# Windowed attention in a fused layer: the softmax division goes from GpSimd onto a diagonal matrix built by VectorE

## Chip, cores and metric

The kernel runs on all 8 cores of one Trainium2 chip. Each core takes one of the 8 sequences (4096 tokens of 1024 features) with the whole set of weights; nothing is exchanged between cores. The metric is device time in microseconds (us) of the slowest core.

## The reference

```python
xn = layernorm(x)                                 # no gain, no bias
q, k, v = split(xn @ w_qkv)                       # 16 heads of 64
s = (q * 64 ** -0.5) @ k.T                        # key j counts for query i if i-255 <= j <= i
a = softmax(s) @ v
g, u = xn @ w_gate.T / 127, xn @ w_up.T / 127     # int32 weights, 3072 hidden
y = x + a @ w_out + (silu(g) * u) @ w_down.T / 127
```

## The kernel before

A core's 32 tiles of 128 tokens are worked in two halves of 16. Each half has an attention phase (A), tile by tile, and then the feed-forward part (phase B) twice, once for each half of the 3072 hidden features. Weights of phase A and of phase B share one region of SBUF, `wreg`: `wq_sb` lies at bytes 0 to 49151 of each partition and `wo_sb` behind it; `wg_sb` (8 pieces of 3072 bytes), `wu_sb` (8 more) and `wd_sb` (12 of 2048 bytes) lie over the same bytes. Loads convert from float32 or int32 to bfloat16 on the way and are issued from the GpSimd queue (`load_attn_weights`, `load_ffn_weights`).

The program is written by hand in the order of the engines' queues. `Sched.add` appends an operation to the queue of one engine and works out its waits from the buffers that it reads and writes; `_wkeys` cuts `wreg` into blocks of 512 bytes, so that a load waits for the last matmul that reads just its own bytes. TensorE alone does not wait for its own earlier work; a VectorE operation that reads a result of VectorE does wait for it.

`phase_a_tile` does this for a tile:

- 128 matmuls (L394) for Q and K in 16 feature chunks of 128 columns (`fc`), 8 matmuls (`d`) each, then 16 of 512 columns for V (L419), which read `wq_sb` row block by row block;
- the transposes of the next tile's normalised input (L369);
- a software pipeline over 8 pairs of heads, in 13 steps. In step s: `pair_softmax` of pair s-1, `pair_scores` of pair s, `pair_transpose` of pair s-3, `pair_av` of pair s-4, and in steps 8 to 12 the output projection (L439).

The score banks are P0 to P4 (head modulo 5), the transposed probabilities go to P5 (even head) and P6 (odd head), the values product to P7. `pair_softmax` has two row maxima on VectorE (L258), two exponentials with their sums on ScalarE (L264), two reciprocals on VectorE (L271) and two multiplications of the 128x384 probabilities by the reciprocals on GpSimd (L277, `mprobs`). `pair_transpose` multiplies each 128x128 block of `mprobs` with the identity (L285) and copies the bank to `probsT`, the even head on ScalarE (L294), the odd on VectorE (L299). `pair_av` ends in a copy to `attnfm` on VectorE (L317). Engines take their queues strictly in order, so VectorE's step is: maximum, maximum, reciprocal, reciprocal, `probsT` copy, `attnfm` copy.

GpSimd's queue holds, for a half: the attention weight loads, the 16 multiplications of each tile, then the feed-forward weight loads, in the order wg piece, wu piece and so on, and wd last.

Of the kernel before, what the change touches and what calls it, by code (L numbers as in the profile page):

```python
# [8 lines left out]
BF16 = mybir.dt.bfloat16  # L9
I32 = mybir.dt.int32  # L10
ALU = mybir.AluOpType
# [9 lines left out]
TILE = 128  # L21
# [15 lines left out]
class Sched:  # L37
# [9 lines left out]
    def add(self, eng, fn, reads=(), writes=(), dma=None):  # L47
        sem = dma if dma else eng
        amt = 16 if dma else 1
        need = {}  # L50

        def req(p):
            s, v = p
            if need.get(s, 0) < v:
                need[s] = v

        for k in reads:
            b = self.buf.get(k)
            if b and b["w"]:
                req(b["w"])  # L60
        for k in writes:
            b = self.buf.get(k)
            if b:
                if b["w"]:
                    req(b["w"])
                for r in b["r"]:
                    req(r)
        kn = self.know[eng]
        waits = []
        for s in sorted(need):  # L70
            v = need[s]
            if (eng == "t" and s == "t") or (dma is not None and s == dma):
                continue
            if kn.get(s, 0) >= v:
                continue
            waits.append((s, v))
            kn[s] = v
            sn = self.snap.get((s, v))
            if sn:
                for s2, v2 in sn.items():  # L80
                    if kn.get(s2, 0) < v2:
                        kn[s2] = v2
        val = self.cnt.get(sem, 0) + amt
        self.cnt[sem] = val
        sn = dict(kn)
        sn[sem] = val
        self.snap[(sem, val)] = sn
        for k in writes:
            self.buf[k] = {"w": (sem, val), "r": []}
        for k in reads:  # L90
            b = self.buf.setdefault(k, {"w": None, "r": []})
            b["r"].append((sem, val))
        self.ops[eng].append((waits, fn, sem, amt))
# [7 lines left out]
def build_program():  # L101
# [13 lines left out]
    A = nc.alloc_sbuf_tensor  # L115
# [14 lines left out]
    qfm = A("qfm", [128, 8, TILE], BF16)  # L130
    attnfm = A("attnfm", [128, 8, TILE], BF16)
    eprobs = A("eprobs", [128, 6, 384], BF16)
    mprobs = A("mprobs", [128, 6, 384], BF16)
    probsT = A("probsT", [128, 6, 384], BF16)
    gsb = A("gsb", [128, HID // 2], BF16)
    usb = A("usb", [128, HID // 2], BF16)
# [4 lines left out]
    id_sb = A("id_sb", [128, TILE], BF16)  # L141
# [11 lines left out]
    recip = A("recip", [128, 6], F32)  # L153
    epsb = A("epsb", [128, 1], F32)

    P = [nc.alloc_psum_tensor(f"P{i}", [128, 512], F32) for i in range(8)]

    sc = Sched(["t", "v", "s", "g", "q"])
    add = sc.add

    add("q", lambda e: e.dma_start(out=id_sb[:], in_=id_d),
        reads=(), writes=("ident",), dma="dc")
    add("q", lambda e: e.dma_start(out=mk_sb[:], in_=mk_d),
        reads=(), writes=("maskadd",), dma="dc")
# [90 lines left out]
    def pair_softmax(t, h0):  # L255
        for h in (h0, h0 + 1):
            bj, pj = h % 5, h % 6
            add("v", (lambda bj, pj: lambda e: e.reduce_max(  # L258
                out=negmax[:, pj:pj + 1], in_=P[bj][:, 0:384], axis=AX.X,
                negate=True))(bj, pj),  # L260
                reads=(f"P{bj}",), writes=(f"nm{pj}",))
        for h in (h0, h0 + 1):
            bj, pj = h % 5, h % 6
            add("s", (lambda bj, pj: lambda e: e.activation(  # L264
                out=eprobs[:, pj, :], in_=P[bj][:, 0:384], func=AF.Exp,
                bias=negmax[:, pj:pj + 1],
                accum_out=sums[:, pj:pj + 1]))(bj, pj),
                reads=(f"P{bj}", f"nm{pj}"), writes=(f"ep{pj}", f"sm{pj}"))
        for h in (h0, h0 + 1):
            pj = h % 6  # L270
            add("v", (lambda pj: lambda e: e.reciprocal(  # L271
                out=recip[:, pj:pj + 1], in_=sums[:, pj:pj + 1]))(pj),
                reads=(f"sm{pj}",), writes=(f"rc{pj}",))
        for h in (h0, h0 + 1):
            pj = h % 6
            ea, rb = broadcast_tensor_aps(eprobs[:, pj, :], recip[:, pj:pj + 1])
            add("g", (lambda pj, ea, rb: lambda e: e.tensor_tensor(  # L277
                out=mprobs[:, pj, :], in0=ea, in1=rb, op=ALU.mult))(pj, ea, rb),
                reads=(f"ep{pj}", f"rc{pj}"), writes=(f"mp{pj}",))

    def pair_transpose(t, h0):
        for c in range(3):
            for h in (h0, h0 + 1):
                pj, bk = h % 6, 5 + (h & 1)
                add("t", (lambda c, pj, bk: lambda e: e.matmul(  # L285
                    P[bk][:, c * 128:(c + 1) * 128],
                    mprobs[:, pj, c * 128:(c + 1) * 128],
                    id_sb[:], start=True, stop=True))(c, pj, bk),
                    reads=(f"mp{pj}", "ident"), writes=(f"P{bk}",))
        for h in (h0, h0 + 1):  # L290
            pj, bk = h % 6, 5 + (h & 1)
            eng = "s" if (h & 1) == 0 else "v"
            if eng == "s":
                add("s", (lambda pj, bk: lambda e: e.activation(  # L294
                    out=probsT[:, pj, :], in_=P[bk][:, 0:384],
                    func=AF.Identity))(pj, bk),
                    reads=(f"P{bk}",), writes=(f"pt{pj}",))
            else:
                add("v", (lambda pj, bk: lambda e: e.tensor_copy(  # L299
                    out=probsT[:, pj, :], in_=P[bk][:, 0:384]))(pj, bk),  # L300
                    reads=(f"P{bk}",), writes=(f"pt{pj}",))
# [82 lines left out]
    def phase_a_tile(t):  # L384
# [62 lines left out]
        for s_ in range(NP + 5):  # L447
            if 1 <= s_ <= NP:
                pair_softmax(t, 2 * (s_ - 1))
            if s_ < NP:  # L450
                pair_scores(t, 2 * s_)
            if 3 <= s_ <= NP + 2:
                pair_transpose(t, 2 * (s_ - 3))
            if 4 <= s_ <= NP + 3:
                pair_av(t, 2 * (s_ - 4))
            for hp in op_sched.get(s_, ()):
                outproj(hp)
# [193 lines left out]
```

How the kernel before makes its waits and increments, by code:

```python
            def run(eng):  # L593
                for waits, fn, sem, amt in sc.ops[ename]:
                    for s_, v_ in waits:
                        eng.wait_ge(sems[s_], v_)
                    ins = fn(eng)
                    ins.then_inc(sems[sem], amt)
                if ename == "q":
                    eng.wait_ge(sems["dy0"], sc.cnt["dy0"])
                    eng.wait_ge(sems["dy1"], sc.cnt["dy1"])
```

## Time and profile before

| what | us |
|---|---|
| median of 2 runs (2507.62 to 2508.25) | 2507.94 |
| the profiled execution | 2508.11 |
| span of its slowest core, core 5 | 2506.5 |
| spans of the eight cores | 2482.9 to 2506.5 |
| TensorE busy on core 5 | 2168.8 (87%) |
| VectorE busy | 985.3 (39%) |
| ScalarE busy | 813.4 (32%) |
| GpSimd busy | 488.5 (19%) |

The trace is of core 5. Its first half runs phase A from about 51 us to 658 us, phase B up to 1250 us; the second half repeats that. The profiled execution's 2508.11 us hold its span of 2506.5 and 1.6 us around it.

### The profile page before, as it was taken

The numbers are of one execution on the slowest core, as the hardware profiler recorded it, in microseconds if no ns is written. First come the engines' busy times: TensorE is split into PE (matmuls) and PEld (weight loads), VectorE is DVE, ScalarE is ACT, GpSimd is POOL, SyncE is SP. The second block draws the span as 40 slices with busy tenths as digits, with TensorE's granted clock in tenths as the row PEclk, the third lists the DMA queues.
The fourth block names the chain that finished last, engine by engine and source line by source line (L and its number), as shares of the span: only waits on it lengthen the run. The fifth ranks groups of instructions, "written<-read, shape, count | busy, mean of one in ns | idle before, by whom it ended". The sixth has DMA issues, their size and how long they took to land.

```text
span 2506.5 us, 45856 instructions; the slowest of 8 cores (2482.9 to 2506.5 us)
## 1 busy us (share of the span) xinstructions
PE 2168.8 (87%) x16400; PEld 1188.7 (47%) x16400; DVE 985.3 (39%) x2371; ACT 813.4 (32%) x1988; POOL 488.5 (19%) x660
## 2 busy tenths in 40 slices
PE   2999899899589995999949899999894999959999
PEld 1555555555234442444425555555551444414444
DVE  1555555555222321223225555555542222212222
ACT  1544544544211220212224544544541222101221
POOL 1433433323400002000013323323324000020000
PEclk9787787787689997999967787787785999979999
DMA  9000000000540007200080000000006200090001
GB/s 161 10 18 19 10 18 19 10 19 18 88 72 1 1 1 123 54 34 35 27 150 19 10 18 16 13 18 16 12 2 105 47 1 1 1 149 36 26 34 43
DMA packets 30460, 91.15 MB, mean 36 GB/s; under 512 B 3488, under 2 KB 3616, under 8 KB 30240
## 3 DMA queue, kind: packets, MB, share of 16 engines
q0 software_dynamic: 20736, 54.54, 13.8%
q1 hardware_dynamic: 4896, 16.91, 2.3%
q10 hardware_dynamic: 4608, 16.78, 1.7%
q8 instruction: 137, 2.24, 0.4%
q14 instruction: 83, 0.68, 0.1%
HBM read 125.96 MB, written 16.78 MB: 57 GB/s over the span
## 4 chain that ended last, share of the span: by engine, by line
PE 82%; DMA 10%; issue 3%; ACT 2%; DVE 2%; POOL 1%; ACTq 0%; another core or an unknown queue 0%; DVEq 0%; POOLq 0%
PE P L476 13%; PE P L516 13%; PE P L469 13%; PE P L394 9%; PE P L285 7%; PE P L439 6%; PE P L240 6%; PE P L249 5%; DMA wu_sb<-wu 5%; PE P L419 4%; PE P L310 4%; DMA wq_sb<-wq 3%; DMA wd_sb<-wd 2%; DVE negmax L258 2%; PE P L501 2%
## 5 line engine op out<-in xcount | busy, mean ns | idle before, releaser
L469 PE MATMUL P<-wg_sb,xnfm 128*128 128x512 bf16 x1536 | 592.6, 386 | 93.4 <-DMA wg_sb<-wg 93.4
L476 PE MATMUL P<-wu_sb,xnfm 128*128 128x512 bf16 x1536 | 592.1, 385 | 41.7 <-DMA wu_sb<-wu 41.7
L277 POOL TENSOR_TENSOR mprobs<-eprobs,recip 128x384 bf16<-128x384 bf16 x512 | 412.2, 826 | 869.7 <-DVE recip L271 845.8
L487 DVE TENSOR_SCALAR usb<-P 128x512 bf16<-128x512 f32 x192 | 132.8, 691 | 819.2 <-PE P L501 649.8
L483 ACT ACTIVATE gsb<-P 128x512 bf16<-128x512 f32 x192 | 114.7, 597 | 888.5 <-PE P L469 888.5
L264 ACT ACTIVATE eprobs<-P,negmax 128x384 bf16<-128x384 f32 x512 | 293.2, 578 | 241.7 <-DVE negmax L258 233.5
L516 PE MATMUL P<-wd_sb,hfm 128*128 128x512 bf16 x1536 | 362.7, 379 | 2.7 <-DMA wd_sb<-wd 2.6
L394 PE MATMUL P<-xnfm,wq_sb 128*128 128x128 bf16 x4096 | 238.8, 221 | 58.2 <-DMA wq_sb<-wq 58.2
L469 PEld LDWEIGHTS P<-wg_sb,xnfm 128*128 128x128 bf16 x1536 | 151.2, 98 | 285.4 <-issue 110.4
L258 DVE TENSOR_REDUCE negmax<-P 128x1 f32<-128x384 f32 x512 | 259.8, 548 | 23.4 <-PE P L249 23.4
L394 PEld LDWEIGHTS P<-xnfm,wq_sb 128*128 128x128 bf16 x4096 | 235.6, 99 | 66.3 <-issue 59.1
L476 PEld LDWEIGHTS P<-wu_sb,xnfm 128*128 128x128 bf16 x1536 | 151.9, 99 | 233.0 <-issue 57.8
L285 PE MATMUL P<-id_sb,mprobs 128*128 128x128 bf16 x1536 | 220.7, 289 | 44.8 <-ACT probsT L294 38.6
L240 PE MATMUL P<-kring,qfm 64*128 64x128 bf16 x1536 | 197.6, 259 | 63.5 <-ACT eprobs L264 59.1
L516 PEld LDWEIGHTS P<-wd_sb,hfm 128*128 128x128 bf16 x1536 | 142.1, 98 | 140.4 <-issue 4.0
L285 PEld LDWEIGHTS P<-id_sb,mprobs 128*128 128x128 bf16 x1536 | 150.6, 131 | 109.7 <-issue 102.7
L249 PE MATMUL P<-id_sb,mk_sb 128*128 128x128 bf16 x1040 | 180.3, 267 | 0.0
L439 PE MATMUL P<-wo_sb,attnfm 128*128 128x512 bf16 x512 | 168.1, 450 | 3.2
L271 DVE RECIPROCAL recip<-sums 128x1 f32<-128x1 f32 x512 | 83.9, 164 | 208.2 <-ACT eprobs L264 205.9
L299 DVE CAST probsT<-P 128x384 bf16<-128x384 f32 x256 | 142.7, 557 | 58.5 <-PE P L285 57.1
L240 PEld LDWEIGHTS P<-kring,qfm 64*128 64x128 bf16 x1536 | 76.0, 100 | 161.8 <-issue 134.4
L294 ACT ACTIVATE probsT<-P 128x384 bf16<-128x384 f32 x256 | 125.3, 489 | 83.0 <-PE P L285 83.0
(47 smaller groups left out, 1541.7 us busy)
## 6 DMA issues: line engine op xcount, KB each, us to landing
xbuf<-x SPq DMA_DIRECT2D x32, 512.0 KB, 3.6
y<-yout ACTq DMA_DIRECT2D x32, 512.0 KB, 2.7
wq_sb<-wq POOLq DMA_DIRECT2D x16, 768.0 KB, 27.9
wg_sb<-wg POOLq DMA_DIRECT2D x32, 384.0 KB, 22.1
wu_sb<-wu POOLq DMA_DIRECT2D x32, 384.0 KB, 24.8
wd_sb<-wd POOLq DMA_DIRECT2D x48, 256.0 KB, 42.8
wo_sb<-wo POOLq DMA_DIRECT2D x16, 256.0 KB, 46.5
mk_sb<-masks SPq DMA_DIRECT2D x1, 96.0 KB, 3.5
```

What stands on the lines that cost most here:

```text
L240: add("t", (lambda c, sl, j, hp, pj, mi: lambda e: e.matmul(P[pj][:, c * 128:(c + 1) * 128], qfm[64 * j:64 * j + 64, hp, :], kring[64 * j: ...
L249: add("t", (lambda c, mi, pj: lambda e: e.matmul(P[pj][:, c * 128:(c + 1) * 128], mk_sb[:, mi, :], id_sb[:], start=False, stop=True))(c, m ...
L258: add("v", (lambda bj, pj: lambda e: e.reduce_max(out=negmax[:, pj:pj + 1], in_=P[bj][:, 0:384], axis=AX.X, negate=True))(bj, pj), reads=( ...
L264: add("s", (lambda bj, pj: lambda e: e.activation(out=eprobs[:, pj, :], in_=P[bj][:, 0:384], func=AF.Exp, bias=negmax[:, pj:pj + 1], accum ...
L277: add("g", (lambda pj, ea, rb: lambda e: e.tensor_tensor(out=mprobs[:, pj, :], in0=ea, in1=rb, op=ALU.mult))(pj, ea, rb), reads=(f"ep{pj}" ...
L285: add("t", (lambda c, pj, bk: lambda e: e.matmul(P[bk][:, c * 128:(c + 1) * 128], mprobs[:, pj, c * 128:(c + 1) * 128], id_sb[:], start=Tr ...
L299: add("v", (lambda pj, bk: lambda e: e.tensor_copy(out=probsT[:, pj, :], in_=P[bk][:, 0:384]))(pj, bk), reads=(f"P{bk}",), writes=(f"pt{pj ...
L394: add("t", (lambda fc, d, bank, ti: lambda e: e.matmul(P[bank][:, (fc % 4) * 128:(fc % 4 + 1) * 128], wq_sb[:, d, fc * 128:(fc + 1) * 128] ...
L439: add("t", (lambda hp, nb: lambda e: e.matmul(P[2 + nb][:, :], attnfm[:, hp, :], wo_sb[:, hp, nb * 512:(nb + 1) * 512], start=(hp == 0), s ...
L469: add("t", (lambda d, nb, ti, gb: lambda e: e.matmul(P[gb][:, :], xnfm[:, d, ti * 128:(ti + 1) * 128], wg_sb[:, d, nb * 512:(nb + 1) * 512 ...
L476: add("t", (lambda d, nb, ti, ub: lambda e: e.matmul(P[ub][:, :], xnfm[:, d, ti * 128:(ti + 1) * 128], wu_sb[:, d, nb * 512:(nb + 1) * 512 ...
L516: add("t", (lambda c, nb, n2: lambda e: e.matmul(P[6 + n2][:, :], hfm[:, c, :], wd_sb[:, c, n2 * 512:(n2 + 1) * 512], start=(c == 0), stop ...
```

## The change

The division by the softmax sum is done by the matmul that transposes. GpSimd no longer multiplies 128x384 probabilities by the reciprocals. VectorE multiplies the 128x128 identity by the reciprocals, one per partition, into `diagr`; the transposing matmul takes the undivided `eprobs` and has `diagr` where the identity stood, so that each row comes out transposed and scaled. The operand that was the identity keeps its size.

```diff
-    mprobs = A("mprobs", [128, 6, 384], BF16)
+    diagr = A("diagr", [128, 6, TILE], BF16)
...
         for h in (h0, h0 + 1):
             pj = h % 6
-            ea, rb = broadcast_tensor_aps(eprobs[:, pj, :], recip[:, pj:pj + 1])
-            add("g", (lambda pj, ea, rb: lambda e: e.tensor_tensor(
-                out=mprobs[:, pj, :], in0=ea, in1=rb, op=ALU.mult))(pj, ea, rb),
-                reads=(f"ep{pj}", f"rc{pj}"), writes=(f"mp{pj}",))
+            add("v", (lambda pj: lambda e: e.tensor_scalar(
+                out=diagr[:, pj, :], in0=id_sb[:],
+                scalar1=recip[:, pj:pj + 1], scalar2=None,
+                op0=ALU.mult))(pj),
+                reads=("ident", f"rc{pj}"), writes=(f"dg{pj}",))
...
                 add("t", (lambda c, pj, bk: lambda e: e.matmul(
                     P[bk][:, c * 128:(c + 1) * 128],
-                    mprobs[:, pj, c * 128:(c + 1) * 128],
-                    id_sb[:], start=True, stop=True))(c, pj, bk),
-                    reads=(f"mp{pj}", "ident"), writes=(f"P{bk}",))
+                    eprobs[:, pj, c * 128:(c + 1) * 128],
+                    diagr[:, pj, :], start=True, stop=True))(c, pj, bk),
+                    reads=(f"ep{pj}", f"dg{pj}"), writes=(f"P{bk}",))
```

VectorE's queue in the attention part of a tile, from step 2 on, before (s is ScalarE's semaphore, t TensorE's, v VectorE's own):

```order
L258 TENSOR_REDUCE negmax<-P 128x1 [waits t] x2
L271 RECIPROCAL recip<-sums 128x1 [waits s] x2
L299 CAST probsT<-P 128x384 [waits t]
L258 TENSOR_REDUCE negmax<-P 128x1 x2
L271 RECIPROCAL recip<-sums 128x1 [waits s] x2
L299 CAST probsT<-P 128x384 [waits t]
L317 CAST attnfm<-P 128x128 [waits t]
```

and the same place now:

```order
L258 TENSOR_REDUCE negmax<-P 128x1 [waits t] x2
L271 RECIPROCAL recip<-sums 128x1 [waits s] x2
L276 TENSOR_SCALAR diagr<-id_sb,recip 128x128 [waits v] x2
L300 CAST probsT<-P 128x384 [waits t]
L258 TENSOR_REDUCE negmax<-P 128x1 x2
L271 RECIPROCAL recip<-sums 128x1 [waits s] x2
L276 TENSOR_SCALAR diagr<-id_sb,recip 128x128 [waits v] x2
L300 CAST probsT<-P 128x384 [waits t]
L318 CAST attnfm<-P 128x128 [waits t]
```

Two scalings of the identity now stand behind each pair of reciprocals, ahead of the `probsT` copy, and each waits for VectorE's own reciprocal.

GpSimd's queue where the last tile of a half goes over into the feed-forward loads, before:

```order
L277 TENSOR_TENSOR mprobs<-eprobs,recip 128x384 [waits g,s,v]
L277 TENSOR_TENSOR mprobs<-eprobs,recip 128x384 [waits s,v]
L195 DMA wg_sb<-wg 128x1536
L202 DMA wu_sb<-wu 128x1536
L195 DMA wg_sb<-wg 128x1536
L202 DMA wu_sb<-wu 128x1536
```

and now, behind the attention weight loads:

```order
L184 DMA wo_sb<-wo 128x1024 x8
L195 DMA wg_sb<-wg 128x1536 [waits dwa0,t]
L202 DMA wu_sb<-wu 128x1536 [waits t]
L195 DMA wg_sb<-wg 128x1536 [waits t]
L202 DMA wu_sb<-wu 128x1536 [waits t]
L195 DMA wg_sb<-wg 128x1536
L202 DMA wu_sb<-wu 128x1536
```

Nothing stands between the two groups of loads any more; the first feed-forward loads now wait for TensorE's matmuls that read the bytes which they overwrite, where before the multiplications ahead of them had already waited for more.

## Rows read from the trace of the kernel before

**Rows 1.** The page: busy time; the chain that ended last, by engine and line.
```profile
PE 2168.8 (87%) x16400; PEld 1188.7 (47%) x16400; DVE 985.3 (39%) x2371; ACT 813.4 (32%) x1988; POOL 488.5 (19%) x660
...
PE 82%; DMA 10%; issue 3%; ACT 2%; DVE 2%; POOL 1%; ACTq 0%; another core or an unknown queue 0%; DVEq 0%; POOLq 0%
```
**Rows 2.** The page, groups: line engine op, shapes, count | busy, mean ns | idle before.
```profile
L277 POOL TENSOR_TENSOR mprobs<-eprobs,recip 128x384 bf16<-128x384 bf16 x512 | 412.2, 826 | 869.7 <-DVE recip L271 845.8
```
**Rows 3.** Timeline of VectorE, one step: start us, us, what, idle before and releaser.
```profile
528.27 0.16 DVE L271 RECIPROCAL recip<-sums 128x1 f32<-128x1 f32 x1 [0.40 <-ACT eprobs L264]
528.37 0.56 DVE L299 CAST probsT<-P 128x384 bf16<-128x384 f32 x1
528.85 0.28 DVE L317 CAST attnfm<-P 128x128 bf16<-128x128 f32 x1
529.05 1.01 DVE L258 TENSOR_REDUCE negmax<-P 128x1 f32<-128x384 f32 x2
...
531.02 0.16 DVE L271 RECIPROCAL recip<-sums 128x1 f32<-128x1 f32 x1 [0.40 <-ACT eprobs L264]
```
**Rows 4.** Timeline of ScalarE in the same step.
```profile
529.69 0.58 ACT L264 ACTIVATE eprobs<-P,negmax 128x384 bf16<-128x384 f32 x1 [1.13 <-DVE negmax L258]
...
530.26 0.57 ACT L264 ACTIVATE eprobs<-P,negmax 128x384 bf16<-128x384 f32 x1
530.72 0.20 ACT L264 ACTIVATION_READ_ACCUMULATOR eprobs<-P,negmax 128x1 f32 x1
```
**Rows 5.** Timeline of VectorE in the first softmax steps of that tile.
```profile
521.54 0.16 DVE L271 RECIPROCAL recip<-sums 128x1 f32<-128x1 f32 x1 [0.40 <-ACT eprobs L264]
521.64 1.02 DVE L258 TENSOR_REDUCE negmax<-P 128x1 f32<-128x384 f32 x2
```
**Rows 6.** Timeline of TensorE at the end of that tile's pipeline.
```profile
535.20 0.54 PE L310 MATMUL P<-probsT,vring 128*64 128x128 bf16 x6
537.23 1.07 PE L285 MATMUL P<-id_sb,mprobs 128*128 128x128 bf16 x6 [1.49 <-ACT probsT L294]
```
**Rows 7.** Timeline of VectorE in the layer norm: two operations that wait for their predecessor.
```profile
548.07 0.15 DVE L332 TENSOR_SCALAR meanb<-sumx 128x1 f32<-128x1 f32 x1
548.33 0.16 DVE L336 TENSOR_TENSOR m2b<-meanb 128x1 f32<-128x1 f32 x1
```
**Rows 8.** Timeline of GpSimd at the end of both halves' attention phases.
```profile
653.14 0.60 POOL L195 DMA_DIRECT2D wg_sb<-wg  x1
...
660.99 0.67 POOL L202 DMA_DIRECT2D wu_sb<-wu  x1
...
1898.66 0.60 POOL L195 DMA_DIRECT2D wg_sb<-wg  x1
```
**Rows 9.** Timeline of TensorE over the last tile of each half and behind it.
```profile
620.49 7.31 PE L394 MATMUL P<-xnfm,wq_sb 128*128 128x128 bf16 x128
627.64 3.62 PE L419 MATMUL P<-wq_sb,xnfm 128*128 128x512 bf16 x16
...
656.61 1.30 PE L439 MATMUL P<-wo_sb,attnfm 128*128 128x512 bf16 x4
...
701.53 0.59 PE L476 MATMUL P<-wu_sb,xnfm 128*128 128x512 bf16 x1 [2.99 <-DMA wu_sb<-wu]
...
1866.01 7.31 PE L394 MATMUL P<-xnfm,wq_sb 128*128 128x128 bf16 x128
```
**Rows 10.** Stretches: engines' busy us, then granted clock, DMA share, GB/s.
```profile
607.60:615.90 8.30, 6.92 (x52) 3.64 (x50) 5.68 (x18) 4.85 (x15) 4.79 (x7) 0.50 0.01 3
615.90:620.50 4.60, 4.50 (x43) 2.18 (x42) 1.80 (x5) 0.98 (x2) 0.38 (x1) 1.00 0.00 0
...
385.70:391.20 5.50, 5.50 (x35) 2.73 (x34) 2.04 (x7) 1.81 (x7) 1.61 (x2) 0.56 0.00 0
...
653.10:701.50 48.40, 11.35 (x53) 3.31 (x51) 3.18 (x7) 0.98 (x2) 14.88 (x29) 0.57 0.97 153
```
**Rows 11.** The chain that ended last, in order of time: two tiles' starts and output projections.
```profile
354.51 7.15 PE P L394 x128
...
385.71 1.82 PE P L439 x4
388.64 1.82 PE P L439 x4
...
393.70 7.15 PE P L394 x128
...
432.09 7.15 PE P L394 x128
...
583.20 7.15 PE P L394 x128
...
614.05 1.82 PE P L439 x4
...
620.66 7.15 PE P L394 x128
```

## The prediction

> **What bounds the kernel now.** The page comes first: TensorE is busy 87% of the span and carries 82% of the chain that ended last, VectorE and ScalarE 2% each, DMA 10% [rows 1]. By that, a change on VectorE and GpSimd would be nearly free. The attention part of a tile has to be read more closely, because a matmul that is stretched over a short wait counts as busy.
>
> The timeline of VectorE is next. From one second reciprocal to the next, 528.27 to 531.02, are 2.75 us, and the link is closed without TensorE: reciprocal, `probsT` copy 0.10 later, `attnfm` copy 0.48 later, row maxima 0.20 later, all with no idle time in front [rows 3]; ScalarE's first exponential starts 0.64 after the first maximum, the second 0.57 later, its sum is read out 0.46 after that, and the second reciprocal starts 0.30 later [rows 3, 4]. 0.10 + 0.48 + 0.20 + 0.64 + 0.57 + 0.46 + 0.30 = 2.75. So the step is set by a loop through VectorE and ScalarE, which start each other; TensorE, at half clock there (0.50 in the stretches of [rows 10]), has a little less work than a step and fills it. The first steps, where no copies stand between, are the same loop: the maxima follow the reciprocal by 0.10 [rows 5]. The loop hands over to TensorE late in the tile: the transposes at 537.23 wait 1.49 us for ScalarE's `probsT` copy [rows 6], and TensorE's own work sets the rest.
>
> The end of a half's attention is next. GpSimd issues the feed-forward loads from 653.14 to 660.99, behind the last multiplication [rows 8]. TensorE is done with the tile at about 657.9, and gets the last up-projection piece at 701.53 [rows 9]; the DMA engines are 0.97 busy all through 653.1 to 701.5 [rows 10]. This wait is bound by the transfer, counted from the first issue.
>
> **What goes: GpSimd's multiplications.** 512 of 826 ns, 412 us busy, with 870 us idle before them [rows 2]. They stand on no loop above: the transposes of a pair come two steps after its multiplications. Worth nothing by themselves. TensorE keeps its work: it has the same six transposes with the same sizes, and `eprobs` is read by them a step and more before ScalarE writes the buffer again.
>
> **What comes: two scalings in the loop.** Each step's two `diagr` operations stand between the second reciprocal and the copy or maximum that closes the loop, and the whole of their time is added. The trace has no bfloat16 operation of one input from SBUF to SBUF, so I bound it. From below: an operation on one element lets the next start after 0.10 us [rows 3]. From above: the 128-element `attnfm` copy out of PSUM lets it start after 0.20 [rows 3]. A pair costs 0.20 to 0.40. Between them lies a wait: the second scaling needs the second reciprocal, and an operation that waits for its predecessor on VectorE starts 0.26 after it (548.07 to 548.33) [rows 7]. The second reciprocal starts at 0, the first scaling at 0.10, the second at 0.26 or later, the copy at 0.37, where it was 0.10. I take 0.27 for the pair, near the lower end because a short operation costs 0.10 and the wait is what makes the rest.
>
> The Trainium skill's page "VectorE: DVE Perf Modes" (The perf-mode tier table) says that a bfloat16 tensor_scalar within SBUF runs at four elements a cycle, and "Vector Engine (DVE) Microarchitecture Reference" (Measured stream behaviour on trn2) has about 75 ns and 1.04 ns per column beside the queue. By these, an estimate: 75 + 32 x 1.04 = 108 ns, 0.22 for a pair and a growth below of 49 us in place of 60. No row here shows that mode.
>
> How often does it count? The pairs 0 to 6 stand ahead of the transposes at 537.23, at least for the odd bank, which follows VectorE's copy: 7 x 0.27 = 1.9 us. The last pair's scalings delay the copy for the next transposes, which have about 0.2 us to spare beside the output projection; I count 0.1. A tile grows by 2.0 us. In the last tile of each half the growth is hidden by the weight load (below); 30 tiles count: +60 us. Bounds: 30 x (7 x 0.20) = 42 and 30 x (7 x 0.40 + 0.1) = 87.
>
> **What moves: the feed-forward loads.** In the new queue they wait only for the bytes that they overwrite. The first gate piece lies over columns that the first 12 of 16 feature chunks read: free about 5.1 us after the Q and K matmuls begin, at 620.49 + 5.1 = 625.6. The others are free while the V matmuls run, 627.64 to 631.2 [rows 9]. Sixteen pieces take 48.4 us, 3.0 each, and are issued 0.52 apart, so the first two keep the DMA engines busy until the rest are free. The stream begins 653.14 - 625.6 = 27.5 us earlier, and the last piece lands at about 674 and not at 701.5. TensorE ends the tile at 657.9 + 2 to 3.5 = 661 and runs only the first matmuls of phase B by 664; the load is still what it waits for, so the 27.5 are all gained. The wd pieces still wait for the output projection, are issued by 664, and queue behind bytes that move until 674: they shift along. The second half has the same distance, 1898.66 - (1866.01 + 5.1) = 27.5 [rows 8, 9]. Together -55 us. Bounds: 0 if the early loads make no way, and 60. The loads for the second hidden half and the attention loads wait for phase B's matmuls as before: nothing.
>
> The skill's "SBUF — State Buffer" (SBUF: two separate sides) warns that a VectorE operation in a two-port mode locks GpSimd out, so that it cannot write descriptors for its DMAs. While the sixteen are issued there are some four scalings; by rows that is under 1 us of delay, by the worst reading of the rule the gain is lost, which is the fourth case below.
>
> **What is late with them: TensorE's clock.** In tile 583.20 to 620.66 (37.5 us) the clock is 0.50 up to 615.9 and 1.00 behind it, 1.9 us after the first output projection at 614.05. In tile 354.51 to 393.70 (39.2 us) the second output projection too runs at half clock (1.82, not 0.97), the return comes about 4.9 us after the first, and the tile is 1.6 us longer [rows 10, 11]. Three of the 30 tiles are of this late kind, and a tile behind one is in between (393.70 to 432.09, 38.4). Tiles of 37.6 us repeat the early return; tiles of other lengths did not. With 39.6 us I see no reason for the early return to stay, so I take between half and two thirds of the way, 0.9 us for each of 28 tiles: +25 us. Bounds 0 and 1.6 x 28 = 45.
>
> **Sum** against the profiled execution's 2508.1: +60 - 55 + 25 = +30, 2538 us. The median of the runs is 2507.94, so the same sum stands against it.
>
> **Rivals.**
>
> 1. The clock comes back as early as before: 2508 + 60 - 55 = 2513. For it: 27 tiles of 30 do so now. Against it: the regular distance went with a regular length.
>
> 2. Slower by over 2%: the scalings run like the PSUM copy, 0.40 a pair, and the late clock return is the rule: 2508 + 87 + 45 - 55 = 2585. Place: behind the second reciprocal of every pair. With the late clock in every tile it decides from a pair of 0.27 us on (30 x 2.0 + 45 - 55 = +50), with the early one from 0.49. Against it: `attnfm` reads PSUM, these read SBUF.
>
> 3. Not slower: a pair costs 0.20 or less, partly under the wait for ScalarE, and the clock stays: 2508 + 42 - 55 = 2495 or below. It decides from 0.24 a pair downward, where 30 x (7 x 0.24 + 0.1) is no more than the 55 gained. For it: the page's figure. Against it: the queue order, which has both scalings after the last wait of the step.
>
> 4. The loads are issued early but not moved early, held by VectorE or by descriptor writing: 2508 + 60 + 25 = 2593. Against it: sixteen issues take only 8 us.
>
> 5. The scalings fall into gaps of VectorE and cost nothing, the loads come early: 2508 - 55 = 2453, faster by over 2%. The closed loop of 2.75 us speaks against it.
>
> **How the numbers follow.** My sum 0.47; rival 1 0.22; rival 2 0.09; rival 3 0.12; rival 4 0.06; rival 5 0.04. A measurement of this kernel tells about 2%, 50 us, from no change. Over 2% slower (2558 on): rivals 2 and 4 and a tail of my own sum, 0.17. Over 2% faster: rival 5, 0.04. Within: 0.79. The range leaves out rivals 2, 4 and 5 in the main: 2498 to 2566.
>
> **What would show it.** In the profile after, a step of the middle of a tile is 3.0 us, not 2.75, with the two scalings between reciprocal and copy and no idle in front of the copy; the first scaling starts 0.10 after the second reciprocal and the second 0.16 after that. A tile from one start of Q and K to the next is 39.6 to 41.2 us. The first gate piece is issued about 5 us after the last tile's Q and K begin, and TensorE gets its last up piece of the first half at about 701.5 + 15 x 2.9 - 27.5 = 717. I am wrong if the step stays 2.75, if the tile grows by under 1.4 us, or if the wait for the loads keeps its 40 us behind the tile.

## The result, and the profile after

The changed kernel takes 1.0164 times the time before, 95% interval 1.0152 to 1.0176. Against the 2508 us of before that is 2549 us: 41 us or 1.6% slower, within the 2% that counted as no change. The profiled execution used below took 2539.3 us, 31 more than that of before; the runs of the kernel before beside it took 2503.4 us, 36 less. In some executions, of either kernel, the cores of a die show a lower granted clock and the time is longer; every time given here is of an execution without that.

The page of that execution (changed kernel, core 6, the slowest): span, busy time of each engine.

```profile
span 2537.7 us, 44658 instructions; the slowest of 8 cores (2520.7 to 2537.7 us)
...
PE 2182.6 (86%) x16400; PEld 1186.0 (47%) x16400; DVE 1072.8 (42%) x2883; ACT 812.3 (32%) x1988; POOL 76.4 (3%) x148
```

GpSimd lost its 412 us of multiplications [rows 2], VectorE gained 87.5 us, and TensorE is busy for 14 us more [rows 1]. None of this tells where 31 us came from. The timeline of VectorE, one step in the middle of a tile, does; it answers to [rows 3].

```profile
528.01 0.16 DVE L271 RECIPROCAL recip<-sums 128x1 f32<-128x1 f32 x1 [0.40 <-ACT eprobs L264]
528.12 0.42 DVE L276 TENSOR_SCALAR diagr<-id_sb,recip 128x128 bf16<-128x128 bf16 x2
528.45 0.55 DVE L300 CAST probsT<-P 128x384 bf16<-128x384 f32 x1
528.92 0.28 DVE L318 CAST attnfm<-P 128x128 bf16<-128x128 f32 x1
529.12 1.01 DVE L258 TENSOR_REDUCE negmax<-P 128x1 f32<-128x384 f32 x2
...
531.09 0.16 DVE L271 RECIPROCAL recip<-sums 128x1 f32<-128x1 f32 x1 [0.40 <-ACT eprobs L264]
```

The step is 3.08 us (528.01 to 531.09), where it was 2.75. Everything but the two scalings is as before: the copy starts 0.44 behind the reciprocal and not 0.10, so a pair of scalings costs 0.33 to 0.34, or 0.17 each, though each is shown lasting 0.25. No operation of VectorE in the step has idle time in front of it but the two reciprocals, which wait for ScalarE: the loop is closed as before, and longer.

The chain that ended last, in order of time: starts of the Q and K part of five tiles, and the first output projection of one. It answers to [rows 11].

```profile
462.36 7.15 PE P L395 x128
...
503.32 7.15 PE P L395 x128
536.46 1.82 PE P L440 x4
544.27 7.15 PE P L395 x128
...
667.26 7.15 PE P L395 x128
...
1312.27 8.67 PE P L395 x124
...
1926.84 7.15 PE P L395 x128
```

Two tiles in a row take 40.96 and 40.95 us (462.36 to 503.32 to 544.27); all 28 between the first and the last of each half take 40.6 to 41.2. From the start of the first tile of the second half to that of the last, 15 tiles, are 614.6 us (1312.27 to 1926.84). The end of such a tile, in the timeline of TensorE and in three stretches (busy us of the engines, then granted clock, DMA share, GB/s), answers to [rows 10]:

```profile
536.40 1.89 PE L440 MATMUL P<-wo_sb,attnfm 128*128 128x512 bf16 x4
538.08 1.00 PE L286 MATMUL P<-diagr,eprobs 128*128 128x128 bf16 x6
...
539.48 1.68 PE L440 MATMUL P<-wo_sb,attnfm 128*128 128x512 bf16 x4
```

```profile
536.40:539.40 3.00, 3.00 (x18) 1.32 (x16) 1.57 (x7) 1.46 (x6) 0.00 (x0) 0.50 0.03 5
539.40:544.20 4.80, 4.70 (x36) 2.03 (x33) 1.71 (x6) 1.68 (x4) 0.00 (x0) 0.85 0.00 0
```

The second output projection now runs mostly at half clock (1.68 for four, against 0.97 at full). Before, full clock came 1.7 to 2.9 us after the start of the first projection in 23 of these 28 tiles, and later in five; now it comes 3.6 to 4.4 us after it. What else the granted clock shows is how long each tile stays at half clock. Before, and then now:

```profile
598.90:615.80 16.90, 15.43 (x120) 8.35 (x121) 11.68 (x36) 9.89 (x32) 10.79 (x14) 0.50 0.01 2
616.00:636.00 20.00, 18.29 (x219) 12.38 (x216) 7.04 (x16) 5.74 (x14) 1.94 (x4) 1.00 0.09 28
```

```profile
520.40:540.70 20.30, 16.28 (x119) 8.34 (x119) 14.08 (x49) 10.17 (x31) 0.00 (x0) 0.50 0.00 1
540.90:561.00 20.10, 18.07 (x225) 12.68 (x223) 9.43 (x25) 8.49 (x19) 0.00 (x0) 1.00 0.10 27
```

By the clock's own record the stretch at half clock lasts 17.1 us in 26 of the 28 tiles before and 20.5 us in the two longest; in the changed kernel it lasts 20.5 us in all 28.

The timeline of GpSimd behind the last tile of both halves, for [rows 8], and of TensorE, for [rows 9]:

```profile
672.77 0.53 POOL L195 DMA_DIRECT2D wg_sb<-wg  x1 [662.63 <-PE P L395]
...
683.33 0.63 POOL L202 DMA_DIRECT2D wu_sb<-wu  x1
```

```profile
667.10 7.31 PE L395 MATMUL P<-xnfm,wq_sb 128*128 128x128 bf16 x128
...
706.65 1.30 PE L440 MATMUL P<-wo_sb,attnfm 128*128 128x512 bf16 x4
...
719.35 0.58 PE L477 MATMUL P<-wu_sb,xnfm 128*128 128x512 bf16 x1 [3.01 <-DMA wu_sb<-wu]
...
1979.12 0.59 PE L477 MATMUL P<-wu_sb,xnfm 128*128 128x512 bf16 x1 [2.16 <-DMA wu_sb<-wu]
```

The first load is issued 5.7 us after the last tile's Q and K part starts and no longer 32.6, and waits for a matmul of that part (L395) alone. Between that issue and the last up piece the DMA engines are 0.99 busy:

```profile
672.80:719.30 46.50, 32.41 (x250) 16.21 (x247) 20.08 (x66) 15.43 (x44) 14.77 (x28) 0.73 0.99 158
```

From that tile's start in the chain to the last up piece are 719.35 - 667.26 = 52.1 us, where it was 701.53 - 620.66 = 80.9.

The second half of the kernel before, for comparison: the starts of its first and last tile in the chain, and the last up piece.

```profile
1295.05 8.73 PE P L394 x124
...
1866.17 7.15 PE P L394 x128
```

```profile
1946.08 0.58 PE L476 MATMUL P<-wu_sb,xnfm 128*128 128x512 bf16 x1 [2.25 <-DMA wu_sb<-wu]
```

The account of the profiled executions, then: up to the start of each half's last tile, +46.6 us in the first half (667.26 against 620.66) and +43.5 in the second (614.6 against 571.1, 1866.17 less 1295.05); from there to the last up piece -28.8 and -27.6. The sum is +33.7, the spans differ by 31.2. The 41 us of the medians are some 7 more, which these two traces do not place.

### The profile page after: what moved, and what is told of

Read it like the earlier page. It is cut to its first block, busy times and chain, and to the rows that moved or that the text cites. A ratio compares the mean times of both kernels' runs of the same rounds, so it can differ in the third digit from the quotient of the medians.

```text
span 2593.2 us, 44486 instructions; the slowest of 8 cores (2522.9 to 2593.2 us)
## 1 busy us (share of the span) xinstructions
PE 2215.5 (85%) x16228; PEld 1199.1 (46%) x16400; DVE 1073.9 (41%) x2883; ACT 814.0 (31%) x1988; POOL 76.4 (3%) x148
## 4 chain that ended last, share of the span: by engine, by line
PE 78%; DMA 9%; DVE 7%; issue 4%; ACT 2%; POOL 1%; DVEq 0%; ACTq 0%; POOLq 0%
PE P L477 13%; PE P L517 13%; PE P L470 12%; PE P L395 9%; PE P L440 6%; PE P L286 6%; PE P L240 5%; PE P L420 4%; PE P L311 4%; PE P L249 3%; DVE probsT L300 3%; DMA wq_sb<-wq 3%; DVE negmax L258 3%; DMA wd_sb<-wd 3%; DMA wu_sb<-wu 3%
## 5 line engine op out<-in xcount | busy, mean ns | idle before, releaser
L477 PE MATMUL P<-wu_sb,xnfm 128*128 128x512 bf16 x1536 | 610.5, 397 | 28.5 <-DMA wu_sb<-wu 23.5
L470 PE MATMUL P<-wg_sb,xnfm 128*128 128x512 bf16 x1472 | 586.0, 398 | 52.9 <-DMA wg_sb<-wg 52.9
L517 PE MATMUL P<-wd_sb,hfm 128*128 128x512 bf16 x1492 | 374.2, 393 | 4.3 <-DMA wd_sb<-wd 1.5
L286 PE MATMUL P<-diagr,eprobs 128*128 128x128 bf16 x1536 | 226.5, 286 | 93.4 <-DVE probsT L300 54.5
L395 PE MATMUL P<-xnfm,wq_sb 128*128 128x128 bf16 x4096 | 239.1, 221 | 58.5 <-DMA wq_sb<-wq 58.5
L395 PEld LDWEIGHTS P<-xnfm,wq_sb 128*128 128x128 bf16 x4096 | 235.9, 99 | 66.6 <-issue 59.5
L286 PEld LDWEIGHTS P<-diagr,eprobs 128*128 128x128 bf16 x1536 | 142.6, 126 | 171.5 <-issue 165.3
L311 PE MATMUL P<-probsT,vring 128*64 128x128 bf16 x1536 | 126.4, 292 | 0.0
```

Of the source, the lines that this page charges most:

```text
L286: add("t", (lambda c, pj, bk: lambda e: e.matmul(P[bk][:, c * 128:(c + 1) * 128], eprobs[:, pj, c * 128:(c + 1) * 128], diagr[:, pj, :], s ...
L311: add("t", (lambda c, sl, j, pj, h, avk: lambda e: e.matmul(P[avk][64 * j:64 * j + 64, 0:128], vring[:, sl, h * 64:(h + 1) * 64], probsT[: ...
L395: add("t", (lambda fc, d, bank, ti: lambda e: e.matmul(P[bank][:, (fc % 4) * 128:(fc % 4 + 1) * 128], wq_sb[:, d, fc * 128:(fc + 1) * 128] ...
L470: add("t", (lambda d, nb, ti, gb: lambda e: e.matmul(P[gb][:, :], xnfm[:, d, ti * 128:(ti + 1) * 128], wg_sb[:, d, nb * 512:(nb + 1) * 512 ...
L477: add("t", (lambda d, nb, ti, ub: lambda e: e.matmul(P[ub][:, :], xnfm[:, d, ti * 128:(ti + 1) * 128], wu_sb[:, d, nb * 512:(nb + 1) * 512 ...
L517: add("t", (lambda c, nb, n2: lambda e: e.matmul(P[6 + n2][:, :], hfm[:, c, :], wd_sb[:, c, n2 * 512:(n2 + 1) * 512], start=(c == 0), stop ...
```

## The experiments

Eight further kernels, and the changed kernel once more, all on eight cores; ratios are to the kernel before, with their 95% intervals.

**Scalings moved into VectorE's wait** (`e_hidden`). Each pair's two scalings leave the place behind their reciprocals and stand, as a function `pair_diag` of their own, behind the next pair's row maxima.

```diff
     def pair_softmax(t, h0):
...
                 reads=(f"P{bj}",), writes=(f"nm{pj}",))
+        if h0 >= 2:
+            pair_diag(t, h0 - 2)
...
-        for h in (h0, h0 + 1):
-            pj = h % 6
-            add("v", (lambda pj: lambda e: e.tensor_scalar(
-                out=diagr[:, pj, :], in0=id_sb[:],
...
                 pair_softmax(t, 2 * (s_ - 1))
+            if s_ == NP + 1:
+                pair_diag(t, 2 * NP - 2)
```

> Changed kernel, but each pair's two scalings stand one step later, behind the next pair's row maxima, where VectorE waits 0.40 us for ScalarE; the last pair's stand at the start of step 9. Same operations, same early loads. Loop theory: two scalings take 0.34 us there and fit the 0.40 us wait, the step falls back to 2.75 us, tiles to about 37.6 us, the clock returns early again, and the 55 us of the loads remain: about 2453 us, ratio 0.98. Rival (the growth comes from what the operations are, or from the transposing matmul with a true second operand, not from where they stand): about as the changed kernel, 2545 us.

Measured: 0.9756 (0.9733 to 0.9778), 2446 us. VectorE's timeline of this kernel, one step:

```profile
525.55 0.16 DVE L282 RECIPROCAL recip<-sums 128x1 f32<-128x1 f32 x1 [0.40 <-ACT eprobs L275]
...
526.32 1.01 DVE L267 TENSOR_REDUCE negmax<-P 128x1 f32<-128x384 f32 x2
527.25 0.41 DVE L258 TENSOR_SCALAR diagr<-id_sb,recip 128x128 bf16<-128x128 bf16 x2
527.73 0.16 DVE L282 RECIPROCAL recip<-sums 128x1 f32<-128x1 f32 x1
528.29 0.17 DVE L282 RECIPROCAL recip<-sums 128x1 f32<-128x1 f32 x1 [0.40 <-ACT eprobs L275]
```

The step is 2.74 us again. The wait in front of the first reciprocal is gone from the row, since the scalings fill it, and the second one's is as before. Nothing was removed from the changed kernel, only moved, and it went from 41 us over to 62 us under the time before. The growth came from the place of the scalings; that the transposing matmul now has a scaled diagonal as its operand costs nothing that shows here. This is the fastest version of the study.

**The diagonal form in the last tile of each half only** (`e_last_only`): the kernel before, with the new lines for `t % HALF_T == HALF_T - 1` and the old ones else.

```diff
+        if t % HALF_T == HALF_T - 1:
+            for h in (h0, h0 + 1):
+                pj = h % 6
+                add("v", (lambda pj: lambda e: e.tensor_scalar(
+                    out=diagr[:, pj, :], in0=id_sb[:],
...
+        else:
+            for h in (h0, h0 + 1):
+                pj = h % 6
                 ea, rb = broadcast_tensor_aps(eprobs[:, pj, :], recip[:, pj:pj + 1])
...
+                if t % HALF_T == HALF_T - 1:
+                    add("t", (lambda c, pj, bk: lambda e: e.matmul(
+                        P[bk][:, c * 128:(c + 1) * 128],
+                        eprobs[:, pj, c * 128:(c + 1) * 128],
+                        diagr[:, pj, :], start=True, stop=True))(c, pj, bk),
+                        reads=(f"ep{pj}", f"dg{pj}"), writes=(f"P{bk}",))
+                    continue
```

> Kernel before, with the diagonal form in the last tile of each half alone; the other 30 tiles keep GpSimd's multiplications. Theory: the loads come early because GpSimd has no work in that tile, and the growth of one tile lies under the load: 2508 - 55 = 2453 us or slightly below. Rival (the loads gain less than they start earlier, since they then meet other work): 2480 to 2508 us.

Measured: 0.9786 (0.9767 to 0.9805), 2453 us, as expected. Thirty tiles are those of before; the loads start earlier, and the growth of the last tile of each half lies under them. The 55 us of the loads are real and need no more than an empty GpSimd queue in two tiles.

**The early loads taken back** (`e_no_early_load`):

```diff
+        if h0 == NH - 2:
+            for h in (h0, h0 + 1):
+                pj = h % 6
+                add("g", (lambda pj: lambda e: e.tensor_tensor(
+                    out=gtmp[:, pj:pj + 1], in0=sums[:, pj:pj + 1],
+                    in1=recip[:, pj:pj + 1], op=ALU.mult))(pj),
+                    reads=(f"sm{pj}", f"rc{pj}"), writes=(f"gt{pj}",))
```

> Changed kernel plus two one-element multiplications on GpSimd behind the last pair's reciprocals of each tile, which hold the feed-forward loads back to where they were. Theory: loses the early loads alone, 2549 + about 55 = 2604 us. Rival (the loads gained nothing and the loop grew less than its rows say): stays near 2549 us.

Measured: 1.0376 (1.0353 to 1.0400), 2602 us. Against the changed kernel's 1.0164 that is 53 us: the loads give it 53 us, and without them it would be 94 us slower than before.

**Every scaling twice** (`e_double`): the loop over the two scalings stands twice.

```diff
+        for h in (h0, h0 + 1):
+            pj = h % 6
+            add("v", (lambda pj: lambda e: e.tensor_scalar(
+                out=diagr[:, pj, :], in0=id_sb[:],
...
```

> Changed kernel with every scaling written twice, so four in the loop. Loop theory: each step 0.34 us longer again, 3.42 us; 7 x 0.34 = 2.4 us more a tile from VectorE. With a clock return that follows the work at a fixed distance: +2.4 x 30 = 72 us, 2621 us. With a clock return that holds tile lengths at certain values: tiles no longer all alike, mean length 42.7 to 43.5 us, total 2600 to 2625 us. Rival (TensorE at half clock sets the step): no change, 2549 us.

Measured: 1.0533 (1.0509 to 1.0557), 2640 us: over the changed kernel by 93 us, and above my 2600 to 2625. The middle of a tile does what was expected, the end does not:

```profile
528.17 0.16 DVE L271 RECIPROCAL recip<-sums 128x1 f32<-128x1 f32 x1 [0.40 <-ACT eprobs L264]
...
528.64 0.42 DVE L283 TENSOR_SCALAR diagr<-id_sb,recip 128x128 bf16<-128x128 bf16 x2
528.98 0.55 DVE L307 CAST probsT<-P 128x384 bf16<-128x384 f32 x1
...
531.62 0.16 DVE L271 RECIPROCAL recip<-sums 128x1 f32<-128x1 f32 x1 [0.40 <-ACT eprobs L264]
```

```profile
532.44 0.31 PE L293 MATMUL P<-diagr,eprobs 128*128 128x128 bf16 x1
533.11 0.69 PE L293 MATMUL P<-diagr,eprobs 128*128 128x128 bf16 x5 [0.36 <-DVE probsT L307]
```

The step is 3.45 us. But behind the first output projection five of the six transposes now wait 0.36 us for VectorE's copy. In the changed kernel no wait is listed there (1.00 for all six, at 538.08 above). I had counted seven pairs; with four scalings the eighth costs 0.36 us too, 11 us in 30 tiles. The tiles of this kernel in the chain range from 42.8 to 45.9 us and are no longer alike; their stretch at half clock is 23.9 us in 22 of 28 where the changed kernel has 20.5.

**One scaling in the loop, one in the wait** (`e_one_in_loop`): the even head's stays behind the reciprocals, the odd head's is issued by `pair_diag`, called as in `e_hidden`.

```diff
+    def pair_diag(t, h0):
+        for h in (h0 + 1,):
...
-        for h in (h0, h0 + 1):
+        for h in (h0,):
             pj = h % 6
             add("v", (lambda pj: lambda e: e.tensor_scalar(
```

> Changed kernel with the even head's scaling left where it is and the odd head's moved behind the next pair's row maxima: one scaling in the loop, not two. VectorE's part: 7 x 0.17 = 1.2 us a tile over the version with none in the loop (2446 us), so 2446 + 30 x 1.2 = 2482 us if the clock's return keeps its distance from the work. Clock theory: tile lengths become irregular and the return is late in some of them, +0.5 us more a tile on average, about 2497 us. Rival (the growth is a threshold and not a dose): 2446 or 2549 us.

Measured: 0.9955 (0.9931 to 0.9979), 2497 us, the value expected. The chain of this kernel, starts of four tiles:

```profile
484.84 7.15 PE P L406 x128
523.60 7.15 PE P L406 x128
563.49 7.15 PE P L406 x128
602.18 7.15 PE P L406 x128
```

Tiles of about 38.7 and 39.8 us take turns, 39.3 on the mean, and so do the stretches at half clock: 17.1 us in 14 of the 28 tiles and 20.5 in the other 14. By the number of scalings in the loop, 0, 1, 2 and 4, the ratios are 0.9756, 0.9955, 1.0164 and 1.0533: 50 to 52 us for each of the first two, 46 for each of the others. VectorE's own part is 30 tiles x 7 pairs x 0.17 = 36 us for one. Beside the rest, 10 to 16 us for one, stands the longer time at half clock, and from two scalings on the eighth pair.

**More TensorE work and nothing on VectorE** (`e_more_pe`): ten further matmuls in each tile of the kernel before.

```diff
+        for d in (0, 1, 2, 3, 4, 5, 6, 7, 0, 1):
+            add("t", (lambda d, ti: lambda e: e.matmul(
+                P[4][:, :],
+                xnfm[:, d, ti * 128:(ti + 1) * 128],
+                wq_sb[:, d, 2048:2560],
+                start=True, stop=True))(d, ti),
...
         for d in range(8):
             for nb in range(2):
```

> Kernel before with 10 further 128x512 matmuls ahead of the V matmuls of each tile (their result is overwritten): 10 x 0.216 = 2.16 us of TensorE work at full clock, nothing on VectorE, ScalarE or GpSimd. If the clock's return keeps its distance from the work, a tile grows by 2.16 us: 2508 + 32 x 2.16 = 2577 us. Clock theory: the tiles go to the same 40.96 us as in the changed kernel, since 37.5 + 2.16 lies between, and the second output projection is at half clock: 28 x 3.1 + 4 x 2.2 = +96 us, 2604 us.

Measured: 1.0371 (1.0319 to 1.0423), 2602 us. The chain of this kernel:

```profile
332.12 1.82 PE P L448 x4
337.12 7.15 PE P L394 x128
...
378.22 7.15 PE P L394 x128
419.26 7.15 PE P L394 x128
```

These two tiles take 41.1 and 41.0 us, from 2.16 us of work, and the 28 between the first and the last of each half 40.5 to 41.1, all with 20.5 us at half clock. The projection at 332.12 is the second of its tile, 5 us ahead of the next tile's start, and runs at half clock. Of the 94 us added, 69 are matmuls (32 x 2.16), and 25 remain for the later return of the clock. The traces bear the division out: on the same core (5), the start of the first output projection comes 2.15 us later in the tile than before on the mean of the 28, and what follows it takes 0.93 us longer, 26 us in all. So that cost does not need the scalings.

**Scalings beside the multiplications** (`e_both`): the kernel before with the two scalings put in front of GpSimd's multiplications, their result unused.

```diff
+        for h in (h0, h0 + 1):
+            pj = h % 6
+            add("v", (lambda pj: lambda e: e.tensor_scalar(
+                out=diagr[:, pj, :], in0=id_sb[:],
...
         for h in (h0, h0 + 1):
             pj = h % 6
             ea, rb = broadcast_tensor_aps(eprobs[:, pj, :], recip[:, pj:pj + 1])
```

> Kernel before with the two scalings added on VectorE at the changed kernel's place, unused, while GpSimd still multiplies and the transposes still read its result. Theory (removing GpSimd's work gains nothing by itself, and the loads stay late): as the changed kernel with late loads, 2602 us. Rival (VectorE's scalings and GpSimd's multiplications hold each other up at SBUF): above 2620 us, with scalings over 0.25 us or multiplications over 0.83 us in the profile.

Measured: 1.1258 (1.1200 to 1.1316), 2826 us. The theory that I had written down missed by 224 us, and the rival holds: the kernel with the same scalings and late loads, but without the multiplications, is `e_no_early_load` with 2602 us. Groups of this kernel, and a step of VectorE beside GpSimd's multiplications:

```profile
L285 POOL TENSOR_TENSOR mprobs<-eprobs,recip 128x384 bf16<-128x384 bf16 x512 | 412.0, 826 | 1186.7 <-DVE recip L272 1156.0 <-ACT eprobs L265 30.7
L277 DVE TENSOR_SCALAR diagr<-id_sb,recip 128x128 bf16<-128x128 bf16 x512 | 335.4, 695 | 0.0
```

```profile
550.93 1.61 POOL L285 TENSOR_TENSOR mprobs<-eprobs,recip 128x384 bf16<-128x384 bf16 x2 [1.98 <-ACT eprobs L265]
```

```profile
551.00 1.58 DVE L277 TENSOR_SCALAR diagr<-id_sb,recip 128x128 bf16<-128x128 bf16 x2
552.51 1.01 DVE L259 TENSOR_REDUCE negmax<-P 128x1 f32<-128x384 f32 x2
```

A scaling lasts 695 ns on the mean where it lasts 253 without multiplications on GpSimd, and the pair shown ends with the two multiplications, which started 0.07 us before it (552.54 and 552.58). The multiplications keep their 826 ns, and VectorE's row maxima behind the scalings their 1.01 us for two. The Trainium skill's page "SBUF — State Buffer" (SBUF: two separate sides) has a port pair that GpSimd shares with a VectorE operation in a two-port mode, held by the one that starts first for its whole instruction while the other waits. The trace agrees in the times; that the scalings run in such a mode no row shows.

**The wait version with late loads** (`e_hidden_late`): `e_hidden` with the two small multiplications of `e_no_early_load`.

```diff
+        if h0 == NH - 2:
+            for h in (h0, h0 + 1):
+                pj = h % 6
+                add("g", (lambda pj: lambda e: e.tensor_tensor(
+                    out=gtmp[:, pj:pj + 1], in0=sums[:, pj:pj + 1],
+                    in1=recip[:, pj:pj + 1], op=ALU.mult))(pj),
...
```

> The version with the scalings in VectorE's wait, plus two one-element multiplications on GpSimd behind the last pair's reciprocals of each tile, so that the feed-forward loads are issued as late as before. GpSimd's large multiplications are gone, the loop has nothing added, the loads gain nothing. Theory (the multiplications stood on no path): the time of the kernel before, 2500 to 2508 us. Rival (part of the 62 us of the hidden version comes from the removed multiplications): 2480 us or less.

Measured: 1.0009 (0.9997 to 1.0021), 2504.5 us beside 2503.4. Without the early loads and without anything in the loop, the removal of 412 us of GpSimd work is worth nothing. With `e_hidden` it also prices the loads once more: 1.0009 - 0.9756 = 0.0253, or 63 us. That is more than the 53 to 55 of the other two. The intervals of these ratios are 3 to 6 us wide to each side, and the trace of `e_hidden` has no tile of the late kind, 37.6 us on the mean of its 28, where that of `e_hidden_late` has 37.8: about 6 us that are not of the loads.

**The changed kernel again** (`changed_again`), for the profile shown above.

> The changed kernel once more beside the runs above, for a profile with all eight cores undisturbed: 2546 to 2550 us, tiles of 40.96 us in both halves.

Measured: the profiled execution took 2539.3 us, 7 below my 2546, beside 2503.4 for the kernel before, which is 5 below its 2508; and the tiles between the first and the last of each half are 40.6 to 41.2 us, not 40.96 in both halves.

## Why the prediction was right

**The bound.** The prediction read a closed loop of 2.75 us through VectorE and ScalarE where the page shows TensorE. Moving the scalings by one place and nothing else took 103 us off (2549 to 2446), which shows it.

**The two scalings.** The term was too small: 0.27 us for a pair, measured 0.33 to 0.34. I let a scaling cost 0.10 and the wait for the second reciprocal make the rest. In fact each costs 0.17 whether or not it has to wait; `e_one_in_loop` has the same 0.17 (459.11 to 459.28) for one alone:

```profile
459.11 0.25 DVE L287 TENSOR_SCALAR diagr<-id_sb,recip 128x128 bf16<-128x128 bf16 x1
459.28 1.01 DVE L267 TENSOR_REDUCE negmax<-P 128x1 f32<-128x384 f32 x2
```

It lies inside the bounds of 0.10 and 0.20, nearer to the copy from PSUM. The estimate of 0.108 worked out from the Trainium skill's page "Vector Engine (DVE) Microarchitecture Reference" (Measured stream behaviour on trn2) was further off: 0.22 for a pair, against my 0.27.

**How often it counts.** Seven pairs is right, and the last pair costs more than the 0.1 us that I gave it. Of the six transposes behind the first projection the second starts 0.31 us behind the first in nearly every tile of the changed kernel, where it was 0.11 before and is 0.67 in `e_double`. So the last pair costs 0.2 us, and a tile grows by 7 x 0.335 + 0.2 = 2.55 us by VectorE, 76 us in 30 tiles where the prediction has 60.

**The loads.** The forecast was -55; -56 in the profile, -53 by `e_no_early_load`, -55 by `e_last_only`, -63 between the two wait versions, some 6 of them luck with the clock. The last piece was expected at about 717 us and came at 719.35. The issue began 27 us earlier, the stream stayed unbroken, and the grown last tile, which ends at 708, is hidden under it. The fourth rival, loads issued early but moved late, is out: the DMA engines are 0.99 busy from 672.8 to 719.3, and once TensorE has freed their bytes the pieces are issued 0.52 us apart (twelve steps from 677.11 to 683.33), as before, with scalings running on VectorE meanwhile.

**The clock.** I expected 25 us. The profile has 90 us of growth up to the last tiles, less 76, which leaves 14. This is a remainder and not a measurement: no run changes the clock alone. The direction is borne out by `e_more_pe`, where TensorE's work alone brings the same late return, and the same 41 us tiles. The reason that I gave, that the early return belongs to one length of tile, is too simple: in `e_one_in_loop` every second tile, of 38.7 us, has an early return too, 2.1 to 2.5 us after the first projection. What the rows show is that the stretch at half clock goes from 17.1 to 20.5 us as tiles grow. Why it takes just these lengths is left open.

**GpSimd's multiplications.** "Worth nothing by themselves" holds (`e_hidden_late`, 1.0009). It was half the story: had they stayed beside the scalings, these would have been nearly three times as long, as in `e_both`. The prediction did not weigh that, and did not need to.

The sum, +76 - 56 + 14 = +34, against the prediction's +60 - 55 + 25 = +30: one term 16 us too small, another 11 too large. That they nearly cancel is luck; the mechanism, the place of the scalings and the loads are not. By the medians the change is +41, 11 above the forecast.

The first rival (early return of the clock kept), the third (a pair of 0.20) and the fifth (scalings in gaps) fail on rows. The second came nearest to being right in its parts: it needs a late clock in every tile, which is so, and a pair of 0.27 us or more, and a pair costs 0.335. It still missed, since it priced a late return at 1.6 us a tile, from the latest tiles of before, and the return is not as late here: the second projection takes 1.3 to 1.7 us for its four matmuls, where it takes 1.9 in those tiles.

## What to carry to other kernels

Before moving work to an engine that is busy 39% of the time, find out whether it sits in a closed loop with another engine: follow one step from an operation to its next instance and add up the starts. In the loop of this kernel every added operation costs its whole start-to-start time, and the remedy was to place the new work in front of the operation that waits, one step later, where it was free. And look at what else stands on the queue of the engine that is relieved: 412 us of arithmetic off the path were worth nothing, while the loads queued behind them gave 55 us, which two tiles' worth of the change would have brought alone.

## What the runs showed of the hardware

A 128x128 bfloat16 scaling by a per-partition scalar, SBUF to SBUF on VectorE, lasts 253 ns and lets the next start after 0.17 us; beside GpSimd's multiplications it lasts 695 ns on the mean, while these keep their 826. In `e_both` that costs 224 us, and it was not expected.

The length of a tile is not simply the sum of what is in it. The kernel before repeats 37.5 to 37.9 us in most tiles, the one with 2.5 us more on VectorE 40.9, the one with 2.16 us more on TensorE the same 40.9, and the one with half of the scalings alternates between 38.7 and 39.8. With the length goes the time that TensorE's granted clock spends at 1.2 and not 2.4 GHz, 17.1 us or 20.5 in the 28 tiles of each of these four and nothing between. Between them a microsecond added to a tile cost about 1.4: 94 us for 69 in `e_more_pe`, 50 for 36 in `e_one_in_loop`.
